# Reordering one loop list: the second attention's weighted sum behind the up run, next to the first one's

## The chip, the cores and the metric

The kernel runs on one core of one Trainium2 chip. The metric is the device time of one execution in microseconds (us), lower is better. Every "pass" below is one step of the kernel's software pipeline, over one block of 256 tokens.

## The reference

The input x is 128 sequences of 32 tokens with 256 features, and cond is one vector of 256 features for each sequence. One layer is computed, all in fp32:

```python
# first attention (16 heads of 16, inside each sequence)
scale, shift = split(cond @ W_emb + b_emb)
xn  = rms_norm(x, g_norm) * (1 + scale) + shift
q, k, v = heads(xn @ W_qkv);  q, k = rms_norm(q, g_q), rms_norm(k, g_k)
o   = softmax(q @ k.T / 4) @ v
hid = o + o @ W_out
# second attention (causal) only steers a small modulator of the gate
a   = attention(rms_norm(hid, ln1_w), Wq, Wk, Wv, Wo)
mod = 0.1 * tanh(a @ A)                       # 16 numbers for each token
h   = rms_norm(hid, ln2_w)
gate = silu(h @ W_in.T + mod * (h @ A) @ B)   # 1024 features
x + hid + (gate * (h @ W_up.T)) @ W_down.T
```

## The kernel before, in words

The 4096 tokens are cut into 16 blocks (n = 0 to 15) of 256 tokens. A block goes through some 118 steps, and the steps of up to five neighbouring blocks are interleaved. The interleaving is one list written out by hand, `ORDER` (lines 35 to 54): each entry is the name of a step and a shift, and in the pass p of the loop the step is done for block p + shift. Every engine walks through the same list and executes only the steps that are its own; so the list gives the order of instructions in the queue of each engine, and semaphores tie the engines together. `START` (line 59) and `END` (line 133) are such lists for filling and draining the pipeline; between them `ORDER` runs for p = 4 to 13 (line 58), ten passes.

Weights and activations of the large products are split into a high and a low fp32r part, so a product over 256 features takes 2 x 3 matmuls (lines 491 to 506). The exact fp32 operations on TensorE are the transposes and the small products of the two attentions. Steps of the part of the list that is touched, by engine:

- TensorE (PE). `a_scores`: 32 small products q by k of the first attention (line 515). `f_up3`, `f_down1`, `f_down2`, `f_up0`, `f_down3`, `f_gate0`: runs of 12 matmuls each of the feed-forward part (line 503 through `feature_major`, line 727 for down), `f_gate0` followed by two matmuls with the modulator (line 713). `b_pv`: weighted sum of the second attention, 32 products of tiles of 128 rows x 32 columns (line 680). `a_pv0`, `a_pv1`: weighted sum of the first attention, tiles of 32 x 32 (line 618). `x_turn`: four transposes of x (line 568). `m_turn`: two transposes of the modulator (line 689). `r_mm` and `a_qk1` (line 495) follow `f_gate0`.
- VectorE (DVE). `a_shift` and `a_rowsum` (lines 923 to 933) are the softmax of the first attention, `a_flip` (line 937) transposes its weights into pTa. `f_mul3` (line 1094) multiplies gate and up, reading the bank `up_bank`. `m_mul` (lines 1075 to 1081, four small instructions) builds the modulator mt. `x_scale` (line 1021) scales x out of `x_bank`. `o_even` (line 1047) and `o_lo` (line 1051) take part in moving the first attention's output to SBUF.
- ScalarE (ACT). `a_exp` (line 819), `f_hi3` (line 889), `m_tanh` (line 874), `o_odd` (line 823), `m_out` (line 879, the turned modulator into mT), `o_hi` (line 827), `x_hi` (line 783, ah), `f_tanh0` (line 884).
- GpSimd (POOL). `a_weigh` (line 1143), `f_lo3` (line 1150), `x_shift` (line 1126), `x_lo` (line 1130, al).
- SyncE (SP) issues the DMAs of the loop; `b_move` (line 474) moves the second attention's v between partitions for `b_pv`.

Waits that matter here, each ahead of the first instruction of its step: `f_up0` waits for `f_mul3` of the block before (line 694), since both use `up_bank`; `a_pv0` for both `a_flip` and `a_v_out`; `b_pv` for both `b_flip` and the moved v (lines 673 to 675); `m_tanh` for `b_pv`; `m_mul` for `m_tanh`; `m_turn` for `m_mul`; `m_out` for `m_turn`; the modulator's matmuls of `f_gate0` for `m_out` (line 709); `x_scale` for `x_turn`; `x_shift`, `x_hi` and `x_lo` each for the one before; `a_qk1` for `x_lo`. The two lines of the loop that all engines run are

```python
for name, shift in ORDER:
    do(name, p + (odd + shift), (odd + shift) % 2)
```

Of the kernel before, what the change touches and what calls it, by code (L numbers as in the profile page):

```python
# [39 lines left out]
    ("b_weigh0", -1), ("a_v", 0), ("b_flip1", -1), ("a_q_out", 0), ("f_tanh3", -2), ("b_flip0", -1),  # L40
    ("a_scores", 0), ("f_hi2", -2), ("f_half3", -2), ("f_up3", -2), ("x_square", 2), ("f_lo2", -2),
    ("a_shift1", 0), ("f_down1", -2), ("a_shift0", 0), ("a_exp1", 0), ("a_v_out", 0), ("f_down2", -2),
    ("a_rowsum1", 0), ("a_exp0", 0), ("a_rowsum0", 0), ("a_weigh1", 0), ("b_pv", -1), ("x_turn", 1),
    ("f_mul3", -2), ("a_weigh0", 0), ("a_flip1", 0), ("f_hi3", -2), ("f_up0", -1), ("m_tanh", -1), ("f_lo3", -2),
    ("a_flip0", 0), ("m_mul", -1), ("a_pv0", 0), ("a_pv1", 0), ("x_scale", 1), ("m_turn", -1), ("x_shift", 1),
    ("o_odd", 0), ("m_out", -1), ("o_even", 0), ("f_down3", -2), ("o_hi", 0), ("f_gate0", -1), ("x_hi", 1),
    ("o_lo", 0), ("x_lo", 1), ("r_mm", 0), ("f_tanh0", -1), ("f_half0", -1), ("a_qk1", 1), ("f_mul0", -1),
    ("r_square", 0), ("a_qk0", 1), ("r_rms", 0), ("a_square1", 1), ("a_copy1", 1), ("f_gate1", -1), ("f_hi0", -1),
    ("f_lo0", -1), ("r_norm0", 0), ("r_norm1", 0), ("f_out", -2), ("a_sum1", 1), ("r_load", 0), ("r_turn", 0),
# [1149 lines left out]
```

## Time and profile before

| | us |
| --- | --- |
| median of 3 runs | 650.26 |
| the three runs | 644.39, 650.26, 651.15 |
| the profiled execution, its own time | 644.05 |
| its span, first to last instruction | 642.2 |
| outside the span | 1.85 |
| mean granted TensorE clock | 0.973 |

All rows and all durations below come from the one profiled execution. The times of single runs lie up to 7 us apart, so the profiled execution is one of the quick ones and not the median. In a timeline row the first number is the start (us from the start of the span), the second the duration of what the row covers; the ends of matmuls are modelled and neighbouring matmuls overlap, so the distance from start to start is what TensorE spends. PE is TensorE's matmul, PEld its weight load.

### The profile page before, as it was taken

What the parts mean: (1) busy time and instruction counts of PE and PEld (TensorE: products, weight loads), DVE (VectorE), ACT (ScalarE), POOL (GpSimd) and SP (SyncE); (2) the same over time, 40 slices, a digit from 0 to 9 for tenths busy, and PEclk for the clock granted to TensorE, in tenths of its full rate; (3) what the DMA queues carried; (4) which work ended last, traced back from release to release, by engine and by line L of the source; (5) the groups of instructions that cost most, each with busy time, mean ns of one, the idle gap of its engine ahead of it and who ended that gap; (6) DMA issues with size and microseconds to landing.
All of it is one profiled execution on the core that took longest, in us unless ns stands there. A gap on an engine that the chain in (4) does not pass through costs nothing.

```text
span 642.2 us, 22552 instructions
## 1 busy us (share of the span) xinstructions
PE 600.8 (94%) x9112; PEld 558.4 (87%) x9128; DVE 462.7 (72%) x1072; ACT 370.0 (58%) x803; POOL 219.9 (34%) x195
## 2 busy tenths in 40 slices
PE   8565789899999999999999999999999999999998
PEld 8444679788999999999999999999999998888997
DVE  4567877677686777777686767777787766976453
ACT  3646656474565748475666757474656657473431
POOL 1221324415152443424242444334242532523131
PEclk9956899899999999999999999999999999999999
DMA  6322200000201002010101001010101010010000
GB/s 180 87 84 82 74 20 23 15 21 17 67 18 50 18 4 60 11 54 15 50 18 51 19 19 45 8 56 13 51 18 50 18 35 15 7 38 16 26 27 34
DMA packets 31977, 24.35 MB, mean 38 GB/s; under 512 B 7648, under 2 KB 30816, under 8 KB 31888
## 3 DMA queue, kind: packets, MB, share of 16 engines
q1 hardware_dynamic: 31200, 22.23, 11.8%
q8 instruction: 73, 1.20, 0.8%
q10 hardware_dynamic: 688, 0.79, 0.4%
q14 instruction: 16, 0.13, 0.1%
HBM read 14.61 MB, written 4.19 MB: 29 GB/s over the span
## 4 chain that ended last, share of the span: by engine, by line
PE 84%; DVE 6%; SPq 3%; issue 3%; ACT 2%; POOL 1%; DMA 1%; DVEq 0%; ACTq 0%; POOLq 0%
PE down_bank L727 13%; PE gate_bank L503 13%; PE up_bank L503 13%; PE b_banks L503 7%; PE a_banks L495 7%; PE x_bank L495 7%; PE a_banks L618 4%; PE b_banks L495 3%; SPq L474 3%; PE a_banks L515 3%; PE b_banks L515 2%; PE gate_bank L713 2%; PE a_banks L591 2%; PE up_bank L542 2%; PE b_banks L680 2%
## 5 line engine op out<-in xcount | busy, mean ns | idle before, releaser
L1150 POOL TENSOR_TENSOR gl<-gu,gh 128x512 fp32r<-128x512 f32 x63 | 81.8, 1300 | 116.0 <-ACT gh L889 115.7
L1087 DVE SCALAR_TENSOR_TENSOR th<-th,gate_bank 128x512 f32<-128x512 f32 x64 | 43.2, 675 | 46.5 <-ACT th L884 46.5
L503 PE MATMUL up_bank<-uh,wup_hi 128*128 128x256 f32 x256 | 76.3, 298 | 0.0
L1136 POOL TENSOR_TENSOR qk<-qk,rx 128x512 f32<-128x512 f32 x32 | 33.3, 1061 | 123.8 <-DVE rx L915 123.8
L727 PE MATMUL down_bank<-wdn_hi,gh 128*128 128x256 f32 x256 | 74.2, 290 | 0.0
L503 PE MATMUL gate_bank<-uh,win_hi 128*128 128x256 f32 x256 | 72.4, 283 | 0.2
L727 PE MATMUL down_bank<-wdn_hi,gl 128*128 128x256 f32 x256 | 72.2, 282 | 0.0
L727 PE MATMUL down_bank<-wdn_lo,gh 128*128 128x256 f32 x256 | 72.1, 282 | 0.0
L503 PE MATMUL up_bank<-ul,wup_hi 128*128 128x256 f32 x256 | 72.0, 281 | 0.0
L503 PE MATMUL up_bank<-uh,wup_lo 128*128 128x256 f32 x256 | 72.0, 281 | 0.0
L503 PE MATMUL gate_bank<-ul,win_hi 128*128 128x256 f32 x256 | 71.5, 279 | 0.0
L503 PE MATMUL gate_bank<-uh,win_lo 128*128 128x256 f32 x256 | 71.5, 279 | 0.0
L1143 POOL TENSOR_TENSOR za<-za,ria 128x512 f32<-128x512 f32 x32 | 33.0, 1052 | 80.4 <-DVE ria L933 80.4
L884 ACT ACTIVATE th<-gate_bank 128x512 f32<-128x512 f32 x64 | 38.3, 598 | 37.7 <-PE gate_bank L713 34.6
L889 ACT ACTIVATE gh<-gu 128x512 fp32r<-128x512 f32 x64 | 40.2, 631 | 27.7 <-DVE gu L1094 19.6
L503 PEld LDWEIGHTS up_bank<-uh,wup_hi 128*128 128x128 f32 x256 | 48.8, 191 | 2.7 <-issue 2.5
L1094 DVE TENSOR_TENSOR gu<-th,up_bank 128x512 f32<-128x512 f32 x64 | 42.9, 670 | 9.4 <-PE up_bank L503 6.6
L503 PEld LDWEIGHTS gate_bank<-uh,win_hi 128*128 128x128 f32 x256 | 48.2, 188 | 1.4 <-issue 0.8
L503 PEld LDWEIGHTS up_bank<-ul,wup_hi 128*128 128x128 f32 x256 | 49.0, 191 | 0.0
L727 PEld LDWEIGHTS down_bank<-wdn_hi,gh 128*128 128x128 f32 x256 | 48.3, 189 | 0.8 <-issue 0.4
L503 PEld LDWEIGHTS up_bank<-uh,wup_lo 128*128 128x128 f32 x256 | 48.7, 190 | 0.0
L503 PEld LDWEIGHTS gate_bank<-ul,win_hi 128*128 128x128 f32 x256 | 48.1, 188 | 0.4
(159 smaller groups left out, 1844.8 us busy)
## 6 DMA issues: line engine op xcount, KB each, us to landing
xa<-in_x SPq DMA_DIRECT2D x16, 256.0 KB, 3.6
xres<-in_x SPq DMA_DIRECT2D x16, 256.0 KB, 3.0
vj<-vs SPq DMA_DIRECT2D x256, 16.0 KB, 1.8
out<-outb SPq DMA_DIRECT2D x15, 256.0 KB, 3.2
stage<-in_w_inT SPq DMA_DIRECT2D x2, 512.0 KB, 3.6
stage<-in_w_upT SPq DMA_DIRECT2D x2, 512.0 KB, 4.1
stage<-in_w_downT SPq DMA_DIRECT2D x2, 512.0 KB, 4.0
stage<-in_w_qkv SPq DMA_DIRECT2D x2, 384.0 KB, 4.9
```

Of the source, the lines that this page charges most:

```text
L495: mm = pe.matmul(dst, stat[a][:, k, t * P:(t + 1) * P], w[b][:, k, c0:c1], start=(k == 0 and j == 0), stop=(k == KT - 1 and j == 2))
L503: mm = pe.matmul(dst, w[a][:, k, c0:c0 + P], mov[b][:, k, :], start=(first and k == 0 and j == 0), stop=(last and k == KT - 1 and j == 2), ...
L515: mm = pe.matmul(place(t, m, b, g), stat(t, m)[rows, 32 * b:32 * b + 32], mov(t, m)[rows, P * b:P * b + P], start=start, stop=True, skip_g ...
L618: mm = pe.matmul(Ab[32 * r:32 * r + 32, b // 2, c:c + 64], vs1[rows, t, hd:hd + 32], pTa[rows, t, hz:hz + 2, :].rearrange("p h s -> p (h s)"),
L727: mm = pe.matmul(Db[:, t * D:(t + 1) * D], stat[a], wdn[b][:, 2 * c + i, :], start=(c + t + i + j == 0), stop=(c == PAIRS - 1 and i == 1 a ...
L884: act.activation(th[:, :, :].rearrange("p c n -> p (c n)"), Gb[:, :], ACT.Tanh, scale=0.5).then_inc(f_tanh, 1)
L889: act.activation(gh[:, c % 2], gu[:, c % 2], ACT.Copy).then_inc(f_hi, 1)
L1087: dve.scalar_tensor_tensor(out=whole, in0=whole, scalar=1.0, in1=Gb[:, :], op0=ALU.add, op1=ALU.mult).then_inc(f_half, 1)
L1094: dve.tensor_tensor(gu[:, c % 2].rearrange("p c n -> p (c n)"), th[:, :, :].rearrange("p c n -> p (c n)"), Ub[:, :], ALU.mult).then_inc(f_ ...
L1136: pool.tensor_tensor(heads_of, heads_of, rx[:, 32 * t:32 * t + 32].unsqueeze(2).to_broadcast([P, 2 * H, HD]), ALU.mult).then_inc(done[name ...
L1143: pool.tensor_tensor(z[:, t], z[:, t], ri[:, t, :].unsqueeze(2).to_broadcast([P, H, S]), ALU.mult).then_inc(done[name], 1)
L1150: pool.tensor_tensor(gl[:, c % 2], gu[:, c % 2], gh[:, c % 2].bitcast(F32), ALU.subtract).then_inc(f_lo, 1)
```

## The change

Only `ORDER` changes, in three of its lines; the same entries stand in another order. No step, wait or buffer is added or removed, and `START` and `END` stay.

```diff
@@ ORDER @@
-    ("a_rowsum1", 0), ("a_exp0", 0), ("a_rowsum0", 0), ("a_weigh1", 0), ("b_pv", -1), ("x_turn", 1),
-    ("f_mul3", -2), ("a_weigh0", 0), ("a_flip1", 0), ("f_hi3", -2), ("f_up0", -1), ("m_tanh", -1), ("f_lo3", -2),
-    ("a_flip0", 0), ("m_mul", -1), ("a_pv0", 0), ("a_pv1", 0), ("x_scale", 1), ("m_turn", -1), ("x_shift", 1),
-    ("o_odd", 0), ("m_out", -1), ("o_even", 0), ("f_down3", -2), ("o_hi", 0), ("f_gate0", -1), ("x_hi", 1),
+    ("a_rowsum1", 0), ("a_exp0", 0), ("a_rowsum0", 0), ("a_weigh1", 0), ("x_turn", 1), ("f_mul3", -2),
+    ("a_weigh0", 0), ("a_flip1", 0), ("f_hi3", -2), ("f_up0", -1), ("f_lo3", -2), ("a_flip0", 0), ("b_pv", -1),
+    ("m_tanh", -1), ("a_pv0", 0), ("a_pv1", 0), ("x_scale", 1), ("m_mul", -1), ("x_shift", 1), ("o_odd", 0),
+    ("o_even", 0), ("f_down3", -2), ("m_turn", -1), ("o_hi", 0), ("m_out", -1), ("x_hi", 1), ("f_gate0", -1),
```

Read by engine, this is:

| engine | before | after |
| --- | --- | --- |
| PE | f_down2, b_pv, x_turn, f_up0, a_pv0, a_pv1, m_turn, f_down3, f_gate0 | f_down2, x_turn, f_up0, b_pv, a_pv0, a_pv1, f_down3, m_turn, f_gate0 |
| DVE | f_mul3, a_flip1, a_flip0, m_mul, x_scale, o_even | f_mul3, a_flip1, a_flip0, x_scale, m_mul, o_even |
| ACT | f_hi3, m_tanh, o_odd, m_out, o_hi, x_hi | f_hi3, m_tanh, o_odd, o_hi, m_out, x_hi |
| POOL, SP | a_weigh1, a_weigh0, f_lo3, x_shift | the same |

## Rows read from the trace of the kernel before

**Rows 1.** Page, part 1: busy us, share of the span, instructions.
```profile
PE 600.8 (94%) x9112; PEld 558.4 (87%) x9128; DVE 462.7 (72%) x1072; ACT 370.0 (58%) x803; POOL 219.9 (34%) x195
```
**Rows 2.** Busy by stretch, the ten passes: PE, PEld, DVE, ACT, POOL, clock, DMA, GB/s.
```profile
191.00:513.20 322.20, 319.83 (x5096) 300.29 (x5108) 244.60 (x578) 199.43 (x441) 123.62 (x109) 1.00 0.11 31
```
**Rows 3.** Waits, 191 to 549 us: us in total, times, longest.
```profile
PEld x_bank L495 <- DVE ul L1068: 2.8, 10, 0.3
```
**Rows 4.** Timeline of PE, one pass around the change; last row: the next pass.
```profile
333.82 0.28 PE L727 MATMUL down_bank<-wdn_hi,gl 128*128 128x256 f32 x1
334.03 0.74 PE L680 MATMUL b_banks<-vj,pTb 128*32 128x16 f32 x64
334.70 0.66 PE L568 MATMUL x_bank<-ident,tok 128*128 128x128 f32 x4
335.11 0.37 PE L503 MATMUL up_bank<-uh,wup_hi 128*128 128x256 f32 x1
...
336.66 1.77 PE L618 MATMUL a_banks<-pTa,vs 32*32 32x64 f32 x128
338.36 0.42 PE L689 MATMUL b_banks<-ident,mt 128*96 128x128 f32 x2
338.54 0.36 PE L727 MATMUL down_bank<-wdn_hi,gh 128*128 128x256 f32 x1
338.74 0.29 PE L727 MATMUL down_bank<-wdn_lo,gh 128*128 128x256 f32 x1
...
369.59 0.28 PE L727 MATMUL down_bank<-wdn_hi,gl 128*128 128x256 f32 x1
```
**Rows 5.** Timeline of DVE, the same pass; last row: f_mul3 of the next.
```profile
329.69 0.69 DVE L923 TENSOR_REDUCE mxa<-a_banks 128x16 f32<-128x512 f32 x1 [0.83 <-PE a_banks L515]
...
334.06 0.68 DVE L1094 TENSOR_TENSOR gu<-th,up_bank 128x512 f32<-128x512 f32 x1
334.66 1.53 DVE L937 STREAM_TRANSPOSE pTa<-za 128x512 f32<-128x512 f32 x2
336.12 0.71 DVE L1075 SCALAR_TENSOR_TENSOR m<-th,ha 128x32 f32<-128x32 f32 x1
...
337.16 0.19 DVE L1081 TENSOR_TENSOR mt<-m,mt 128x32 f32<-128x32 f32 x1
...
369.84 0.63 DVE L1094 TENSOR_TENSOR gu<-th,up_bank 128x512 f32<-128x512 f32 x1
```
**Rows 6.** Timeline where PE waits for DVE in this loop.
```profile
313.09 0.69 DVE L1068 TENSOR_TENSOR ul<-x_bank,uh 128x512 fp32r<-128x512 f32 x1 [0.95 <-ACT uh L845]
...
313.89 0.19 PEld L495 LDWEIGHTS x_bank<-wqkv_hi,uh 128*128 128x128 f32 x1 [0.29 <-DVE ul L1068]
...
313.92 0.36 PE L495 MATMUL x_bank<-wqkv_hi,uh 128*128 128x272 f32 x1
```
**Rows 7.** Timelines of PE ahead of and behind the loop: other neighbours of these steps.
```profile
134.09 0.41 PE L713 MATMUL gate_bank<-mT,b 96*128 96x256 f32 x2
134.33 0.60 PE L568 MATMUL x_bank<-ident,tok 128*128 128x128 f32 x4
134.69 0.36 PE L503 MATMUL b_banks<-uh,wqkv_hi 128*128 128x256 f32 x1
...
577.78 1.18 PE L515 MATMUL b_banks<-k2p,q2T 64*32 64x128 f32 x64
578.89 0.85 PE L618 MATMUL a_banks<-pTa,vs 32*32 32x64 f32 x64
```
**Rows 8.** Timeline of all engines: from the modulator's copy to a_qk1.
```profile
339.05 0.37 ACT L879 ACTIVATE mT<-b_banks 96x256 fp32r<-96x256 f32 x1
...
340.51 0.61 ACT L783 ACTIVATE ah<-xm 128x512 fp32r<-128x512 f32 x1
...
341.20 1.29 POOL L1130 TENSOR_TENSOR al<-xm,ah 128x512 fp32r<-128x512 f32 x1 [1.81 <-ACT ah L783]
...
343.12 0.39 PE L495 MATMUL a_banks<-wqkv_hi,ah 128*128 128x512 f32 x1
```

## The prediction

> **What bounds the kernel now.** I read the page's busy shares first, then the busy time by stretch, the waits of the loop, and last the timelines of one pass. PE is busy 94% of the span, the next engine 72% [rows 1]; in the ten passes of the loop PE is busy 319.83 of 322.20 us at full granted clock [rows 2]. So the loop is PE's instruction stream, one pass lasting 369.59 - 333.82 = 35.77 us, and whatever makes PE start its next run later is paid in full, once a pass, ten times. In the waits the reader should look for two things. PE itself waits for another engine in nearly one place only, for `ul` ahead of `b_v0`, 2.8 us in ten waits, 0.3 us a pass [rows 3]; and DVE begins the first attention's softmax after 0.83 us of waiting for PE's scores, so there DVE has caught up with PE, and its work up to `f_mul3` hangs rigidly on PE's clock [rows 5]. Everything else PE needs is ready when it comes, and the question is whether that stays true once the steps move.
>
> **PE's own work, without waits.** I take the distance from start to start [rows 4].
> - Before: last matmul of `f_down2` at 333.82; `b_pv` 334.03 to 334.70 = 0.67; `x_turn` to 335.11 = 0.41; `f_up0` to 336.66 = 1.55; both `a_pv` to 338.36 = 1.70; `m_turn` to 338.54 = 0.18; then `f_down3`. From 333.82 to the start of `f_down3`: 4.72 us.
> - After: a transpose run behind 128-row fp32r matmuls starts without a gap: at 134.09 two matmuls take 0.24, that is 0.12 each, and `x_turn` then takes 0.36 to the next run [rows 7]. So 0.12 + 0.36 + 1.55 + `b_pv` 0.67 + 1.70 = 4.40 us to the start of `f_down3`.
> - `m_turn` now stands between `f_down3` and `f_gate0`. It keeps its 0.18, and the run behind it pays the slow first matmul that follows an fp32 step: 338.54 to 338.74 = 0.20 in place of 0.12 [rows 4]. `f_down3` itself stands behind an fp32 step in both orders. That adds 0.26.
> - Sum: 4.40 + 0.26 - 4.72 = -0.06 us a pass. The moved `b_pv` saves next to nothing beside `a_pv`.
>
> The one unknown of this sum is the seam from `b_pv` to `a_pv`, which the trace of before does not have. What a seam costs is seen at `f_down2` to `b_pv`: 0.21 from start to start (333.82 to 334.03) where two matmuls of one run are 0.12 apart, so 0.09; the next step begins 0.07 before the last matmul's end (333.82 + 0.28 = 334.10). The same 0.07 stands between the end of `b_pv` (334.03 + 0.74 = 334.77) and `x_turn` (334.70), so the 0.67 of `b_pv` holds a seam already [rows 4]. And two steps of small tiles side by side have it too: the second scores (64x32) end at 577.78 + 1.18 = 578.96 and the first half of a weighted sum (32x32) starts at 578.89, again 0.07 before [rows 7]. I therefore leave `b_pv` at 0.67. At best there is no seam, 0.09 less, at worst a double one, 0.09 more: +-0.9 us over ten passes.
>
> The Trainium skill has a rule on this seam: "TensorEngine Tiling (Array Packing)", section Key Properties, says that changing the tiling mode, and not only the tile, drains the engine. 128x32 and 32x32 are two modes, so by it the two weighted sums still drain between them and the sum stays; were they one mode, it would be 0.9 us less. The row of the scores agrees with the rule.
>
> **The wait that the move uncovers.** `f_up0` may overwrite `up_bank` only when DVE's `f_mul3` has read it. Before, `f_mul3` ends at 334.06 + 0.68 = 334.74 and `f_up0` starts at 335.11, behind `b_pv` and `x_turn` [rows 4, 5]: these two steps cover DVE's softmax. After, PE could start `f_up0` at 333.82 + 0.12 + 0.36 = 334.30, but `f_mul3` does not come earlier: from the first reduction (329.69) to its end DVE works through nine instructions one behind the other, no row between them with idle time, and the first of them waits for PE's `a_scores`, which does not move [rows 5]. How fast PE follows DVE is seen at `b_v0`: DVE ends at 313.09 + 0.69 = 313.78, the weight load starts at 313.89 and the matmul at 313.92, 0.14 later [rows 6]. So `f_up0` starts at 334.74 + 0.14 = 334.88, a stall of 0.58 us. In the next pass `f_mul3` ends at 369.84 + 0.63 = 370.47, PE could start at 369.59 + 0.48 = 370.07 and starts at 370.61: 0.54. Odd and even passes alternate so over all ten; mean 0.56.
>
> The wait blocks PE's whole queue: behind `f_up0` stand `b_pv`, `a_pv`, `f_down3`, all ready or ready soon, and nobody else runs them. And it can't be won back later in the pass, since the next softmax again starts from PE's next `a_scores`.
>
> **The other edits, with what hides them.** Relative to 333.82, `f_up0` starts at +1.06 (before +1.29), `b_pv` at +2.61, `a_pv` at +3.28 = 337.10 (before 336.66). `a_pv` needs `a_flip0`, done at 334.66 + 1.53 = 336.19 [rows 5]: hidden. `a_pv` ends at 338.80, 0.44 later than before.
> - `m_tanh`, `m_mul`: their input is there at 337.10, and ACT has nothing else to do. `m_tanh` is a small ACT step (at most the 0.37 of `m_out` [rows 8]), `m_mul` takes 337.16 + 0.19 - 336.12 = 1.23 [rows 5]: done by 338.8. DVE's next step `o_even` needs `o_odd`, which ACT can't start before `a_pv` ends at 338.80: hidden by the whole of `o_odd`. Uncovered it would delay `o_even`, and with it `r_mm`, one for one.
> - `x_scale` moves ahead of `m_mul`, some 1.2 us earlier; `x_hi`, behind it by way of `x_shift`, stands behind `o_hi` in ACT's queue in either case: 0.
> - `m_turn` comes at 338.80 + 1.52 (twelve matmuls and the slow first) = 340.3, `mt` is there at 338.8: no wait. `m_out` takes the place that `x_hi` had right behind `o_hi`, 340.51 - 338.36 = 2.15 behind the end of `a_pv` [rows 4, 8]: 340.95 to 341.32. `f_gate0` needs it only after its twelve matmuls, at 340.32 + 0.18 + 1.52 = 342.0: hidden by 0.7 less a latency of 0.14.
> - `x_hi` now has `m_out` ahead of it. It comes 0.37, less some 0.09 if it overlaps its neighbour as DVE's do (334.06 + 0.68 = 334.74 against 334.66 [rows 5]: 0.08), so some 0.28, later in relation to `a_pv`. Before, `x_lo` ends at 341.20 + 1.29 = 342.49 and `a_qk1` starts at 343.12, 0.63 later [rows 8]. After, 0.63 - 0.28 + 0.08 (slow first matmul of `f_gate0`) = 0.43, less the latency of 0.14: 0.29 is left. This is the thinnest cover; a miss costs what is missing, each pass.
> - SP and POOL keep their order. The DMAs of `b_move` get 2.4 us more time before `b_pv`: no loss, and no gain unless one was late.
>
> **Sum.** (0.56 - 0.06) x 10 = +5.0 us. `START` and `END` do not change. The profiled execution: 644.05 + 5.0 = 649.1 us (span 642.2 + 5.0, and 1.85 around it). The median of the runs shown is 6.2 us above that execution, and a median of the changed kernel should stand in the same relation: 650.26 + 5.0 = 655.3 us, 0.8% slower. What a measurement of this kernel can tell from no change is about 1%, so this is likely to read as no change.
>
> **Rivals.**
> 1. The stall is there and a second wait joins it (chance 0.12): `a_qk1` for `x_lo`, at ACT's `x_hi`. For: the cover is only 0.29 us and three engines take part. Against: every term of it has a row. It decides once `x_lo` slips by over 0.29; a slip by `m_out`'s length, 0.37, costs 0.08 a pass, one by the length of `x_hi`, 0.61, costs 0.32: 5.0 + 0.8 to 3.2, 656.1 to 658.5 us.
> 2. Not slower (0.08): DVE's release comes before PE needs it, so no wait appears at `f_up0` and only the seams count. Place: DVE's queue between `a_scores` and `f_mul3`; price: -0.06, with the best seam -0.15, a pass, so 648.8 to 649.7 us. It decides if these nine DVE instructions were 0.56 us shorter. For: the bank and the queue would be in the same state, and profiled ends include a tail. Against: `b_v0` shows PE does wait to 0.14 behind such an end [rows 6], and DVE has no slack there [rows 5].
> 3. The stall is about half (0.10): DVE's instructions run faster while PE is not using the other banks, or the first weight load is done during the wait. 10 x (0.28 - 0.06) = +2.2: 652.5 us. For: odd passes show `f_mul3` 0.05 shorter; against: nothing shows 0.28.
>
> **Chances.** The forecast has 0.70. Its own range is +3.5 to +6.5 us (seam +-0.9, stall +-0.05 a pass). Single runs of the kernel lie from 644.39 to 651.15, so it is not sure that the median stands where it stood. The low end is an execution like the profiled one with the smallest own range, 644.05 + 3.5 = 647.5; it takes in rivals 2 and 3. The high end is the median with rival 1's upper end, 658.5. Faster by over 1%: 0.03, which only scatter gives. Slower by over 1% (6.5 us): rival 1 and a fifth of the forecast's cases, 0.26. Within 1%: 0.71.
>
> **What would show it.** Right: the waits of the changed kernel have a new line, PE (or its weight load) at `up_bank` for DVE's `gu`, ten times, some 0.4 to 0.6 us each; a pass lasts 35.77 + 0.50 = 36.27 us; `b_pv` covers 0.67 to the start of `a_pv`; `x_turn` takes 0.36; DVE's distance from the first reduction to the end of `f_mul3` stays at 5.05. Wrong: no such line, or a pass at 35.7 (rival 2); a new wait of PE at `a_banks` line 495 for POOL's `al`, or at `gate_bank` line 713 for `mT` (rival 1); a stall under 0.4 us (rival 3).

## The result, and the profile after: 3% slower, not 0.8%

The changed kernel takes 668.9 us (median of 5 runs, 664.08 to 671.56) against 651.15 us before (median of 5, 644.39 to 652.03): ratio 1.0303, 95% interval 1.0255 to 1.0351. The forecast was 655.3 us, range 647.5 to 658.5. The sign and the forecast stall were right; about four fifths of the loss inside the loop come from something that the prediction does not contain.

**The forecast wait is there.** The waits of the loop in the changed kernel (191 to 560 us; us in total, times, longest):

```profile
PE a_banks L618 <- issue: 7.8, 5, 1.7
...
PE up_bank L503 <- DVE gu L1094: 3.3, 10, 0.4
```

The last line is the forecast one, ten times. But the first is new as well: TensorE stops inside the first attention's weighted sum, five times, up to 1.7 us, and "issue" says that nothing in the profile released it. First the step that went as forecast, the first pass of the loop, timeline of PE and DVE (answers to [rows 4, 5]):

```profile
193.76 0.28 PE L727 MATMUL down_bank<-wdn_hi,gl 128*128 128x256 f32 x1
...
193.88 0.60 PE L568 MATMUL x_bank<-ident,tok 128*128 128x128 f32 x4
194.00 0.68 DVE L1094 TENSOR_TENSOR gu<-th,up_bank 128x512 f32<-128x512 f32 x1
...
194.83 0.36 PE L503 MATMUL up_bank<-uh,wup_hi 128*128 128x256 f32 x1 [0.35 <-DVE gu L1094]
...
196.36 0.74 PE L680 MATMUL b_banks<-vj,pTb 128*32 128x16 f32 x64
...
197.03 1.77 PE L618 MATMUL a_banks<-pTa,vs 32*32 32x64 f32 x128
...
198.73 0.39 PE L727 MATMUL down_bank<-wdn_hi,gh 128*128 128x256 f32 x1
```

`x_turn` starts 0.12 behind the down run; `f_mul3` ends at 194.00 + 0.68 = 194.68 and `f_up0` starts 0.15 later, so 0.95 us lie between the starts of `x_turn` and `f_up0` where 0.36 are needed: 0.59 of stall. `b_pv` takes 0.67, `a_pv` 1.70. These are the forecast terms (`x_turn`'s 0.36 is the forecast's own; under the stall this trace can't show what `x_turn` needs). Now the second pass of the loop:

```profile
233.19 1.45 PE L618 MATMUL a_banks<-pTa,vs 32*32 32x64 f32 x98
...
236.27 0.45 PE L618 MATMUL a_banks<-pTa,vs 32*32 32x64 f32 x30 [1.64 <-issue]
...
236.99 0.42 PE L727 MATMUL down_bank<-wdn_lo,gh 128*128 128x256 f32 x1
...
237.21 0.41 PE L727 MATMUL down_bank<-wdn_hi,gl 128*128 128x256 f32 x1
```

The 128 matmuls of `a_pv` are cut in two: 98, then a stop, then 30. Behind it the matmuls of the down run are 0.22 apart and not 0.12. The busy time by stretch of 1 us tells why (PE, PEld, DVE, ACT, POOL busy, then the granted clock, DMA share, GB/s):

```profile
232.00:233.00 1.00, 1.00 (x62) 0.87 (x62) 0.91 (x2) 0.00 (x0) 0.87 (x1) 1.00 0.00 0
233.00:234.00 1.00, 1.00 (x94) 0.85 (x82) 0.46 (x1) 0.20 (x1) 0.91 (x1) 1.00 0.06 16
234.00:235.00 1.00, 0.58 (x37) 0.37 (x34) 0.64 (x4) 0.00 (x0) 0.13 (x1) 1.00 0.00 0
235.00:236.00 1.00, 0.00 (x0) 0.00 (x0) 0.00 (x0) 0.00 (x0) 0.00 (x0) 1.00 0.00 0
236.00:237.00 1.00, 0.73 (x32) 0.64 (x33) 0.00 (x0) 0.17 (x1) 0.00 (x0) 0.86 0.00 0
237.00:238.00 1.00, 1.00 (x6) 1.00 (x6) 0.44 (x1) 0.52 (x1) 0.00 (x0) 0.50 0.09 16
238.00:239.00 1.00, 1.00 (x7) 1.00 (x6) 0.31 (x1) 0.63 (x1) 0.00 (x0) 0.50 0.00 0
239.00:240.00 1.00, 1.00 (x7) 0.99 (x7) 0.69 (x1) 0.00 (x0) 0.00 (x0) 0.50 0.00 0
240.00:241.00 1.00, 1.00 (x9) 1.00 (x9) 0.00 (x0) 0.90 (x2) 0.02 (x1) 0.93 0.00 0
```

From 235 to 236 no engine does anything: nobody is waiting for a slow neighbour, TensorE itself has nothing to execute. Then its granted clock falls to 0.50, which is 1.2 GHz, for some 3.4 us. And two small transfers stand out, rows with 16 GB/s, begun at 233.9 and 237.8. They belong to the queue that the page calls "instruction":

```profile
q8 instruction: 73, 1.20, 0.8%
```

73 transfers of 1.20 MB in all are 16 KB each. The trace has 18,682 instructions of TensorE (9128 matmuls, 9128 weight loads, 426 that wait or signal), so a transfer stands for 256 of them, 64 bytes each. I conclude that TensorE gets its instructions in blocks of 256 and that this queue brings them; the experiments below test it, and the run with 256 more instructions (64 extra matmuls) has 74 transfers. The same line stands in the page of before; I had not looked at it.

**Where the time went.** The starts of the first attention's scores mark the passes. After, then before:

```profile
188.42 1.16 PE L515 MATMUL a_banks<-k1p,q1T 64*32 64x128 f32 x64
224.62 1.16 PE L515 MATMUL a_banks<-k1p,q1T 64*32 64x128 f32 x64
264.09 1.16 PE L515 MATMUL a_banks<-k1p,q1T 64*32 64x128 f32 x64
300.29 1.16 PE L515 MATMUL a_banks<-k1p,q1T 64*32 64x128 f32 x64
```
```profile
185.47 1.16 PE L515 MATMUL a_banks<-k1p,q1T 64*32 64x128 f32 x64
221.18 1.16 PE L515 MATMUL a_banks<-k1p,q1T 64*32 64x128 f32 x64
```

- Passes 1, 3, 5, 7, 9: 36.20 to 36.24 us, where before they took 35.71 to 35.88; together 181.09 against 178.80, +0.46 a pass. This is the forecast loss (+0.50), by itself.
- Passes 2, 4, 6, 8, 10: 39.47, 39.28, 40.62, 39.62 and 36.45 (the last runs into `END`) against 35.71, 35.71, 35.71, 36.02 and 33.30: +18.99 us. Less 5 x 0.46 for the wait, 16.7 us remain. The five stops themselves are 1.5 to 1.9 us (8.9 in sum); the other 7.8 I put down to the half clock behind each, 3.4 us long and in pass 6 6.8 us. In pass 2: `a_pv` 3.46 for 1.70, then down 2.69 for 1.52, `m_turn` 0.28 for 0.14, gate 1.73 for 1.50.
- Loop: +21.3 us. Ahead of the first scores the profiled execution is 2.95 us later, behind the loop 0.6 us quicker; together the 23.6 us between the two profiled executions. The 2.95 is scatter and no effect of the change: in the seven other kernels traced, all with the same `START` or the few extra matmuls in it, this mark lies between 187.97 and 191.62 us, whatever the order of the loop. The profiled execution of before was the quick one.

### The profile page after: what moved, and what is told of

It reads as the page before. It is cut to its first block, busy times and chain, and to the rows that moved or that the text cites. A ratio compares the mean times of both kernels' runs of the same rounds, so it can differ in the third digit from the quotient of the medians.

```text
span 665.8 us, 22568 instructions
## 1 busy us (share of the span) xinstructions
PE 614.9 (92%) x9128; PEld 569.3 (86%) x9128; DVE 461.9 (69%) x1072; ACT 371.7 (56%) x803; POOL 219.7 (33%) x195
## 4 chain that ended last, share of the span: by engine, by line
PE 71%; DVE 13%; issue 5%; SPq 3%; ACT 2%; POOL 1%; DMA 1%; DVEq 0%; ACTq 0%
PE gate_bank L503 13%; PE down_bank L727 10%; PE up_bank L503 9%; PE b_banks L503 7%; PE x_bank L495 6%; PE a_banks L495 6%; PE a_banks L618 4%; SPq L474 3%; DVE mxa L923 3%; PE b_banks L495 3%; PE a_banks L515 3%; PE b_banks L515 2%; PE gate_bank L713 2%; PE a_banks L591 2%; DVE rsa L931 2%
## 5 line engine op out<-in xcount | busy, mean ns | idle before, releaser
L727 PE MATMUL down_bank<-wdn_hi,gh 128*128 128x256 f32 x256 | 76.8, 300 | 0.0
L503 PE MATMUL gate_bank<-uh,win_hi 128*128 128x256 f32 x256 | 74.5, 291 | 0.2
L727 PE MATMUL down_bank<-wdn_hi,gl 128*128 128x256 f32 x256 | 74.6, 292 | 0.0
L727 PE MATMUL down_bank<-wdn_lo,gh 128*128 128x256 f32 x256 | 74.5, 291 | 0.0
L727 PEld LDWEIGHTS down_bank<-wdn_hi,gh 128*128 128x128 f32 x256 | 50.4, 197 | 1.9 <-issue 0.7
L727 PEld LDWEIGHTS down_bank<-wdn_hi,gl 128*128 128x128 f32 x256 | 50.9, 199 | 0.0
L727 PEld LDWEIGHTS down_bank<-wdn_lo,gh 128*128 128x128 f32 x256 | 50.7, 198 | 0.0
L503 PEld LDWEIGHTS gate_bank<-uh,win_lo 128*128 128x128 f32 x256 | 49.5, 193 | 0.0
```

The lines of the kernel that those rows point to most:

```text
L503: mm = pe.matmul(dst, w[a][:, k, c0:c0 + P], mov[b][:, k, :], start=(first and k == 0 and j == 0), stop=(last and k == KT - 1 and j == 2), ...
L727: mm = pe.matmul(Db[:, t * D:(t + 1) * D], stat[a], wdn[b][:, 2 * c + i, :], start=(c + t + i + j == 0), stop=(c == PAIRS - 1 and i == 1 a ...
```

## The experiments

I set two theories against each other. Theory A: the two weighted sums side by side are a burst of 384 TensorE instructions in 2.4 us (`b_pv` 128, `a_pv` 256: each matmul has a weight load, and fp32 doubles both), and TensorE stops where the next block of 256 has not arrived. Then the place of the stops is set by where the borders of the blocks fall, counted from the start of the program. Two passes have 2308 instructions, 9 x 256 + 4, so the borders fall in the same place of every second pass, two matmuls earlier each time. The stops of the changed kernel stand in front of matmul 98, 96, 94, 92, 90 (counted from 0) of `a_pv` in passes 2, 4, 6, 8, 10: exactly so. Theory B: the pairing or the wait does it, or something else that every second pass does (a transfer, a buffer's turn), and the place of the code in the program does not matter. The test is to shift the whole loop by instructions that do nothing.

### Extra instructions ahead of the old order: 49 and 64 tiny matmuls

```diff
-    ("lo", 1), ("own", 0), ("warm", 0), ("warm", 0), ("m_mm", 0), ("ln1_quarter", 0), ("x_shift", 0),
+    ("lo", 1), ("own", 0), ("warm", 0), ("warm", 0), ("fill", 0), ("m_mm", 0), ("ln1_quarter", 0), ("x_shift", 0),
...
+                elif name == "fill":
+                    for i in range(49):
+                        pe.matmul(Ub[32 * (i % 4):32 * (i % 4) + 32, 0:R], mt[:, 0, 0:32], mt[:, 0, 0:R], start=True, stop=True, skip_group_check=True)
```

> The order of before, with 49 tiny extra matmuls (196 more TensorE instructions) once, in START, where TensorE waits anyway. Their results are never read. Theory A (TensorE fetches its instructions in blocks of 256, and a block that it runs through in less than about 3.5 us makes it wait for the next one): the borders of the blocks now fall so that a whole block lies inside the first attention's weighted sum (256 instructions in 1.7 us) in every other pass. Expected: a stop of about 1.8 us there with no releaser, five times, each followed by some 3.5 us at half clock, and +12 to +17 us in all. Theory B (the stops of the changed kernel come from the two weighted sums standing side by side, or from the wait at up_bank, and have nothing to do with where the code lies): the loop is as before, +0 to +2 us for the extra work.

> The control of the run with 49: the order of before with 64 tiny extra matmuls in START, 256 instructions, one whole block, so that the borders of the blocks fall on the same instructions of the loop as before. Theory A: as before within 2 us. Theory B: the same, 0 to +2 us. If both runs with extra matmuls are slower by the same amount, it was the extra work.

Measured: with 64 (a whole block) 650.32 us against 650.48, ratio 0.9997 (0.9972 to 1.0022), no difference. With 49, 653.36 us, ratio 1.0049 (1.0013 to 1.0085): slower by half a per cent, though the extra work is less. The place of the stops is theory A's to the instruction. Shifted by 196 instructions, the border should move from matmul 98, 94, 92, 90 in passes 2, 6, 8, 10 by 98 back, or by 30 on: to 128 (the end of `a_pv`), 124, 122, 120. The stop of pass 2 stands right behind `a_pv`, that of pass 6 in front of 124. Timeline of the weight loads with 49, passes 8 and 10 (each pair is `a_pv1`, behind the 64 of `a_pv0`):

```profile
451.85 0.64 PEld L618 LDWEIGHTS a_banks<-pTa,vs 32*32 32x32 f32 x58 [0.22 <-PE a_banks L618]
453.10 0.15 PEld L618 LDWEIGHTS a_banks<-pTa,vs 32*32 32x32 f32 x6 [0.61 <-issue]
...
524.59 0.63 PEld L618 LDWEIGHTS a_banks<-pTa,vs 32*32 32x32 f32 x56 [0.22 <-PE a_banks L618]
525.78 0.15 PEld L618 LDWEIGHTS a_banks<-pTa,vs 32*32 32x32 f32 x8 [0.57 <-issue]
```

64 + 58 = 122 and 64 + 56 = 120. And the old order, without extra work, has such stops too, at the border the theory gives for pass 10 (90):

```profile
515.59 1.35 PE L618 MATMUL a_banks<-pTa,vs 32*32 32x64 f32 x90
517.11 0.64 PE L618 MATMUL a_banks<-pTa,vs 32*32 32x64 f32 x38 [0.16 <-issue]
```

But the size was expected wrong. I had reckoned 12 to 17 us, with stops of 1.8 us, for a block that lies wholly inside the 1.7 us of `a_pv`; they were 1.3, 0.3, 0.7 and 0.6 us in passes 2, 6, 8 and 10, and no fall of the clock followed any of them. The time that a block is given is not the only thing; what stands ahead of the burst counts as well (below).

Nor are the stops all that this run loses. In its trace `b_pv` also waits for the moved v, four times, 2.2 us in sum (0.1 us in the trace of before, 0.7 with 64); the longest wait:

```profile
376.40 0.72 PE L680 MATMUL b_banks<-vj,pTb 128*32 128x16 f32 x64 [0.88 <-DMA vj<-vs]
```

In the trace of before the last piece of v lands as little as 0.13 us ahead of `b_pv`, so the old order has next to no slack there; in the changed kernel, behind the up run, it is 1.9 us or more. In the run with 49 all four waits fall in passes with a block border in `a_pv`, but no run shows whether the place of the borders causes them.

### Extra instructions ahead of the changed order: 32 and 17

The same `fill` with `range(32)` and `range(17)` in the changed kernel.

> The changed order with 32 tiny extra matmuls in START (128 TensorE instructions, half a block), results never read. Theory A (blocks of 256 instructions): the borders fall into the other passes. The long stops without a releaser move from the even-numbered to the odd-numbered passes of the loop (the first, third, fifth ...), in front of matmul 99, 97, 95, 93, 91 of the 128 of the first attention's weighted sum, and there are none over 0.5 us in the other five; the time stays that of the changed kernel, 3% over before. Theory B (something that every second pass does, such as a transfer or a buffer's turn, makes the stop): the stops stay in the second, fourth ... pass and in front of the same matmuls as they were.

Measured: 667.9 us against 647.96, ratio 1.0327 (1.026 to 1.0394). The stops moved to passes 1, 3, 5, 7, 9, in front of matmul 99 (counted from 0) and then 97, 95, 93, 91; passes 2, 4, 6, 8, 10 have none. Timeline, passes 1 and 2:

```profile
197.95 1.48 PE L618 MATMUL a_banks<-pTa,vs 32*32 32x64 f32 x99
201.16 0.45 PE L618 MATMUL a_banks<-pTa,vs 32*32 32x64 f32 x29 [1.73 <-issue]
...
235.93 1.77 PE L618 MATMUL a_banks<-pTa,vs 32*32 32x64 f32 x128
```

The same loop, the same data and the same transfers of data, and the stops change passes: theory B is out. Every second pass stops because every second pass has its border there. That the two sums must also stand side by side for stops of this length, the runs below show.

> The changed order with 17 tiny extra matmuls in START (68 TensorE instructions). Theory A: borders fall in front of matmul 64, 62, 60, 58, 56 in passes 2, 4, 6, 8, 10, with the border before them at the start of the second weighted sum, behind the slow up run: stops of 0.2 to 0.8 us there, as in the run with 49 extra matmuls in the old order. In passes 1, 3, 5, 7, 9 they fall at the end of the first weighted sum (matmul 127, 125, ...) with the border before them inside the pair: stops of 1.3 to 1.9 us and half clock behind them. Time: as the changed kernel, -1 to +4 us. Theory that only the pairing counts and not where the borders lie: stops unchanged, in front of matmul 98 to 90.

Measured: 665.65 us, ratio 1.0256 (1.0191 to 1.0322). Both kinds of stop appear. The short ones stand in front of matmul 64, 62, 60, 58, 56 as expected; the long ones came one step later than expected, in pass 1 in front of the second matmul of the down run, then in front of 127, 125, 123, 121 in passes 3 to 9. Passes 2 and 3:

```profile
237.65 0.86 PE L618 MATMUL a_banks<-pTa,vs 32*32 32x64 f32 x64
239.17 0.85 PE L618 MATMUL a_banks<-pTa,vs 32*32 32x64 f32 x64 [0.67 <-PE a_banks L618]
...
274.41 1.75 PE L618 MATMUL a_banks<-pTa,vs 32*32 32x64 f32 x127
277.90 0.24 PE L618 MATMUL a_banks<-pTa,vs 32*32 32x64 f32 x1 [1.74 <-issue]
```

(The first stop is put down to a matmul, since `a_pv1` has a wait for `a_pv0` just there; in passes 4 to 10 the stops of this kind, in front of 62 to 56, fall inside `a_pv0`.) Behind the short kind, 0.7 to 0.9 us, the clock stayed at 1.00. Behind the long kind, 1.7 to 1.95 us, it fell to 0.50 in passes 1 and 3 alone, and not in 5, 7 and 9, where I had expected it too. Busy time by stretch around the stops of passes 2 and 3, and behind that of pass 5:

```profile
238.30:239.20 0.90, 0.23 (x27) 0.07 (x8) 0.81 (x4) 0.00 (x0) 0.31 (x1) 1.00 0.00 0
239.20:240.60 1.40, 1.40 (x69) 1.31 (x70) 0.00 (x0) 0.53 (x1) 0.00 (x0) 1.00 0.06 12
...
277.90:278.50 0.60, 0.60 (x3) 0.53 (x4) 0.00 (x0) 0.32 (x1) 0.00 (x0) 0.74 0.00 0
278.50:281.00 2.50, 2.50 (x15) 2.49 (x13) 1.41 (x2) 0.99 (x2) 0.00 (x0) 0.50 0.03 7
...
354.40:358.40 4.00, 3.99 (x35) 3.90 (x36) 1.44 (x2) 2.30 (x5) 0.65 (x1) 1.00 0.02 4
```

This separates the two parts of the cost. Passes 1 and 3, with the fall, took 39.41 and 39.65 us, passes 5, 7 and 9, without it, 37.97 to 38.15: the slow clock costs some 1.5 us a time, the stop itself some 1.8 over the 36.2 us of a pass without one. The run with 32 has such a pass too, pass 1: a stop of 1.96 us, 38.06 us in all, and the clock at 1.00 behind it:

```profile
201.20:205.20 4.00, 4.00 (x60) 3.91 (x61) 1.44 (x2) 2.21 (x5) 0.49 (x1) 1.00 0.02 4
```

**What sets the length of a stop.** For five stops I took from the traces when TensorE executed the border before, when the transfer on the instruction queue began, and when work went on:

| stop | border before | transfer begins | stops | goes on | from transfer |
| --- | --- | --- | --- | --- | --- |
| changed order, pass 2 | 232.8, in `b_pv` | 233.9 | 234.4 | 236.27 | 2.4 |
| with 17, pass 3 | 274.3, end of `b_pv` | 275.2 | 275.9 | 277.90 | 2.7 |
| with 17, pass 2 | 237.0, start of `b_pv` | 236.7 | 238.3 | 239.17 | 2.5 |
| old order with 49, pass 8 | 450.1, end of the up run | 450.5 | 452.5 | 453.10 | 2.6 |
| old order, pass 10 | 513.3, in `b_pv`, an up run follows | 514.5 | 516.7 | 517.11 | 2.6 |

A block is usable 2.4 to 2.7 us after its transfer begins in these five. Over all 39 stops of 0.3 us and more at such borders in the loops of the nine traces it is 2.2 to 2.8 us, and 1.2 to 1.6 us after the transfer has ended, so each stop ends at a nearly fixed distance from the transfer of its block. The beginning of the transfer goes with the border before, but not at a fixed distance. With that border in or right behind the up run (the rows with 49 and with 17, pass 2) it begins 0.3 us before to 0.5 behind the border's execution; with it inside `b_pv` or at its end, 0.9 to 1.2 behind. My explanation is that whatever reads the instructions is ahead of the array behind a stretch of large matmuls, and not inside the burst; I conclude it from these five, and no run isolates it. It would explain why 256 instructions in 1.7 us cost 0.2 to 1.3 us behind an up run and 1.5 to 2.1 us behind `b_pv`: the burst of 384 is long enough to hold two borders.

The Trainium skill, "Runtime: NRT & Kernel Launch", section Instruction fetch mechanics, has this queue: instructions come in blocks of 16 KiB, which are 256 instructions, and the next block is fetched while the current one is executed. That agrees with the 73 transfers. It calls the cost of crossing a border "mostly hidden"; here it is so in the trace of before (stops of 0.3 and 0.4 us, in two of ten passes) and not in the changed kernel (1.5 to 1.9 us in five).

### One part of the change at a time

`pv_only`: in the list of before, `("b_pv", -1)` stands ahead of `("a_pv0", 0)`; all else stays.

```diff
-    ... ("b_pv", -1), ("x_turn", 1), ... ("f_up0", -1), ... ("m_mul", -1), ("a_pv0", 0),
+    ... ("x_turn", 1), ... ("f_up0", -1), ... ("m_mul", -1), ("b_pv", -1), ("a_pv0", 0),
```

> One part of the change alone: the second weighted sum moved behind the up run, right ahead of the first; modulator and x's scaling stay as before. If the move of that one step carries the loss: the wait for gu at up_bank (0.3 to 0.6 us, ten times), the stops in front of matmul 98 to 90 in every second pass, and the changed kernel's time within 3 us, that is +15 to +21 us against before. If the reordering of modulator and scaling had a share, it would be clearly nearer to before.

Measured: 665.59 us against 647.96, ratio 1.0294 (1.0216 to 1.0372): the whole loss. Waits of the loop (190 to 570 us):

```profile
PE a_banks L618 <- issue: 8.0, 5, 1.8
...
PE up_bank L503 <- DVE gu L1094: 3.6, 10, 0.4
```

`a_pv_back`: in the changed list `("b_pv", -1)` back ahead of `("x_turn", 1)`.

> The changed order with the second weighted sum put back ahead of x_turn: only the reordering of modulator and x's scaling is left. My steps: no wait at up_bank, no stop; m_turn between down and gate costs 0.04 to 0.1 a pass: +0.3 to +1 us. If m_out ahead of x_hi, or m_turn behind the down run, had a share in the loss, it would be over +3 us, with a new wait of TensorE for al or mT.

Measured: 649.96 us, ratio 0.9997 (0.9963 to 1.0032). The reordering of the modulator and of x's scaling costs nothing that can be measured, and brings no wait for `al` of over 0.2 us and none for `mT`. So the thin cover of `x_hi` held. "No stop" did not hold: at the borders of passes 2, 6, 8 and 10 TensorE stops for 0.3, 0.7, 0.6 and 0.3 us, at full clock, and `b_pv` waits for the moved v in three passes, 1.2 us in sum. That is the size of the stops in the old order, with the up run between the two sums.

`mid`: in the list of before `("b_pv", -1)` between `("f_hi3", -2)` and `("f_up0", -1)`, so behind `x_turn` and ahead of the up run.

> One entry moved against before: the second weighted sum stands between x_turn and the up run. It still covers the time that VectorE needs for f_mul3, and the two weighted sums are kept apart by the up run. Theory A with the wait of my prediction: no wait for gu at up_bank, no stop of over 0.7 us, a pass shorter by 0.1 (seams), so -1.5 to +2 us. Theory that the stop comes from the pairing of the two sums alone predicts the same; a theory that any move of the second sum behind x_turn costs would have it some 10 to 20 us slower.

Measured: 647.95 us, ratio 0.9973 (0.994 to 1.0005): no wait for gu, stops of 0.2 to 0.9 us (I had expected none over 0.7), all at borders, clock at 1.00 behind them. It is within the scatter of before; a pass takes 35.76 and not the 35.6 that I expected of the seams, since `x_turn` takes 0.53 us to the start of `b_pv` in nine of the ten passes, not 0.36. So the second sum may stand on either side of `x_turn`. What costs is the other side of the up run. No version tried is clearly quicker than before.

## Why the prediction was wrong, step by step

- *The wait that the move uncovers*: right in place, count and size. 0.59 and 0.53 us in passes 1 and 2 against 0.58 and 0.54 forecast, ten times, and DVE's stretch from first reduction to the end of `f_mul3` stayed at 194.68 - 189.63 = 5.05. Five passes without a stop are 0.46 longer, forecast 0.50.
- *The seams*: right. `b_pv` to `a_pv` is 0.67, the value with a seam, also where no stop follows; that agrees with the rule of the Trainium skill that changing the tiling mode drains the engine ("TensorEngine Tiling (Array Packing)", Key Properties), though no run has the two sums in one mode. `m_turn` alone took 0.14 and not 0.18. `x_turn`'s 0.36 can't be seen under the stall.
- *The other edits, with what hides them*: right as far as can be told, by the run that has them alone (`a_pv_back`, 0.9963 to 1.0032, so to some 2 us).
- *PE's own work, without waits*: this is the step that failed. "I take the distance from start to start [rows 4]" makes a step cost the same wherever it stands. It held for what the array and the other engines do, and not for the supply of instructions, a term that the sum does not have: 384 small ones in 2.4 us were more than the queue brought, and the up run between the two sums [rows 4] was what gave it time. With the burst whole, every second pass loses some 3.3 us, 16.7 in all where the sum has nothing, of which about half is the clock that falls behind the five stops. The measured loss inside the loop is 21.3 us, not 5.0.
- None of the *rivals* named it. Rival 1 had the right sign and the wrong place (`a_qk1`, +0.8 to 3.2 us). The range of +3.5 to +6.5 us for the change itself had no room for it.
- The trace of before had the sign of it: the waits of PE over the whole span list `a_banks` line 618 with "issue", 0.7 us in two times. One of the two is the stop in front of matmul 90 in pass 10. I took "a wait with no releaser" for noise.
- Carrying the sum over to the median was not safe either. The profiled execution of before lay 6 to 7 us below its median, that of the changed kernel 1.3 us below, so the medians differ by 17.75 us and the profiled executions by 23.6. The 2.95 us ahead of the loop are a part of it; no trace of a slower execution of before is there to show the rest.

## What to carry to other kernels

Before two runs of tiny matmuls are put side by side, count the instructions, not only the time: here a block of 256 TensorE instructions run through in 1.7 us or less, with nothing slow ahead of it, outran the instruction queue. A stretch of large matmuls between two such bursts is cover for the fetch, just as it is cover for another engine; and a step that is moved away takes its cover with it (here `b_pv` covered VectorE's softmax). A stop that hits every second pass, in front of a matmul that moves by a constant from one to the next, points at the position of the code: shift the code by some dummy instructions, here 128, to prove it before looking in the buffers.

## What the runs showed of the hardware that I had not expected

- TensorE's instructions come in blocks of 256 on a queue of their own (73 transfers of 16 KB); a block was usable 2.2 to 2.8 us after its transfer began, though the transfer itself took 0.9 to 1.5 us.
- A stop's cost can nearly double through the clock, and it is not sure to. Stops of up to 0.9 us ran on at 1.00, and the one of 1.34 us (49 extra matmuls, pass 2) did too. Of the 20 stops of 1.5 to 2.1 us in the four kernels with the two sums side by side, 16 came with a stretch of 3.4 us or more at 0.50 (1.2 GHz) that began at most 1.3 us after work went on; four, of 1.7 to 2.0 us, ran on at 1.00. What decides between them is open.
- Dummy instructions once, some 165 us ahead of the loop, make the kernel 0.5% slower (49) or not (64), with the same work in the loop: part of a measured difference between two versions can be the position of the code alone.
